# Criss-cross attention on one core: attention matmuls of 96 columns and 96 partitions instead of 128

## The reference

```python
q = jnp.einsum('oc,bchw->bohw', Wq, x) + bq[None, :, None, None]   # 64 channels
k = jnp.einsum('oc,bchw->bohw', Wk, x) + bk[None, :, None, None]   # 64 channels
v = jnp.einsum('oc,bchw->bohw', Wv, x) + bv[None, :, None, None]   # 512 channels
energy_H = jnp.einsum('bchw,bcgw->bhwg', q, k)
energy_H = energy_H - NEG * eye[None, :, None, :]
energy_W = jnp.einsum('bchw,bchv->bhwv', q, k)
att = jax.nn.softmax(jnp.concatenate([energy_H, energy_W], axis=-1), axis=-1)
att_H, att_W = (att[..., :H], att[..., H:])
out_H = jnp.einsum('bcgw,bhwg->bchw', v, att_H)
out_W = jnp.einsum('bchv,bhwv->bchw', v, att_W)
return gamma * (out_H + out_W) + x
```

## Time and profile before

| | |
|---|---|
| median of 2 runs | 4363.76 us (4362.07 to 4365.45) |
| profiled execution, span from first to last instruction | 4357.4 us |
| mean granted TensorE clock | 0.936 |
| TensorE busy with matmuls | 93% of the span |
| weight loads | 84% |
| VectorE, ScalarE, GpSimd busy | 50%, 30%, 26% |
| DMA | 947.78 MB, mean 218 GB/s |

### The profile page before, as it was taken

The page is one execution under the profiler, slowest core; times in us unless marked ns, Lnnn a source line. Parts: engine busy times, 40 slices in busy tenths (PEclk is TensorE's granted clock), DMA queues, the critical chain, the costliest instruction groups (busy, mean ns, idle before and its releaser), DMA issues.

```text
span 4357.4 us, 92393 instructions
## 1 busy us (share of the span) xinstructions
PE 4063.6 (93%) x26136; PEld 3654.3 (84%) x26136; DVE 2184.9 (50%) x3932; ACT 1288.8 (30%) x2522; POOL 1148.6 (26%) x1006
## 2 busy tenths in 40 slices
PE   8989999898998999989999899997999979999897
PEld 7878988788887998879988699886988869988697
DVE  3348533485334853348433484335843358433584
ACT  3342133421334213341133411335113351133510
POOL 3322133221332213322233222332223322233211
PEclk9988999889998999979999799997999979999799
DMA  5548977489774897749977499774997749977499
GB/s 177 172 150 213 247 231 244 153 219 253 232 238 146 222 256 229 247 136 229 249 236 239 136 232 245 246 238 134 234 239 243 240 137 232 252 237 232 148 243 315
DMA packets 555124, 947.78 MB, mean 218 GB/s; under 512 B 45120, under 2 KB 383552, under 8 KB 533568
## 3 DMA queue, kind: packets, MB, share of 16 engines
q1 hardware_dynamic: 555072, 947.30, 75.2%
HBM read 550.77 MB, written 396.36 MB: 217 GB/s over the span
## 4 chain that ended last, share of the span: by engine, by line
PE 82%; DMA 9%; issue 3%; ACT 2%; SPq 1%; POOL 1%; DVE 0%; ACTq 0%; POOLq 0%; DVEq 0%
PE bank L708 36%; PE bank L766 26%; PE bank L724 9%; DMA Pe<-e_scratch 7%; PE bank L745 5%; PE bank L734 3%; PE bank L755 3%; ACT kq L461 1%; DMA KQ<-kq_scratch 1%; POOL Pe L388 1%; ACT E L466 1%; DMA kq_scratch<-kq 1%; POOL x_split L372 0%; SPq L224 0%; DVE X L608 0%
## 5 line engine op out<-in xcount | busy, mean ns | idle before, releaser
L708 PE MATMUL bank<-Wv_hi,x_split 128*128 128x512 f32 x4608 | 1525.6, 399 | 0.0
L766 PE MATMUL bank<-Pt,V 128*128 128x128 f32 x12288 | 1478.4, 280 | 0.0
L766 PEld LDWEIGHTS bank<-Pt,V 128*128 128x128 f32 x12288 | 1436.7, 196 | 0.0
L608 DVE TENSOR_TENSOR X<-bank,X 128x384 f32 (+1 forms) x1536 | 1115.4, 734 | 559.1 <-PE bank L766 559.0
L372 POOL TENSOR_TENSOR x_split<-X,x_split 128x768 fp32r<-128x768 f32 x384 | 702.3, 1854 | 1411.1 <-ACT x_split L435 1411.0
L555 DVE TENSOR_TENSOR v_out<-bank,bv_row 128x512 f32<-128x512 f32 x576 | 398.3, 691 | 1287.3 <-PE bank L708 1281.2
L708 PEld LDWEIGHTS bank<-Wv_hi,x_split 128*128 128x128 f32 x4608 | 867.9, 188 | 189.0 <-issue 0.5
L708 PE MATMUL bank<-Wv_lo,x_split 128*128 128x512 f32 x2304 | 912.5, 396 | 0.0
L388 POOL TENSOR_TENSOR Pe<-Pe,mx 96x384 f32<-96x384 f32 x384 | 316.6, 824 | 1288.6 <-DMA Pe<-e_scratch 1287.8
L474 ACT ACTIVATE Pt<-bank 96x384 f32<-96x384 f32 x384 | 187.3, 488 | 1424.9 <-PE bank L755 1424.9
L446 ACT ACTIVATE kq<-bank,bqk_sb 64x192 f32<-64x192 f32 x768 | 320.6, 417 | 812.1 <-PE bank L734 645.8
(11 more groups left out here) (45 smaller groups left out, 1551.9 us busy)
## 6 DMA issues: line engine op xcount, KB each, us to landing
V<-v_scratch SPq DMA_DIRECT2D x384, 768.0 KB, 5.7
X<-in_x SPq DMA_DIRECT2D x192, 768.0 KB, 5.1
v_scratch<-v_out SPq DMA_DIRECT2D x576, 256.0 KB, 3.8
out<-X SPq DMA_DIRECT2D x192, 768.0 KB, 6.3
Pe<-e_scratch SPq DMA_DIRECT2D x384, 144.0 KB, 5.3
kq_scratch<-kq SPq DMA_DIRECT2D x384, 96.0 KB, 2.3
e_scratch<-E SPq DMA_DIRECT2D x384, 72.0 KB, 1.7
e_scratch<-E SPq DMA_DIRECT2D x192, 144.0 KB, 1.9
```

The costliest lines, as they stand in the source:

```text
L608: nc.vector.tensor_tensor(xs, o_ps[r][:, :].rearrange("p (t n) -> p t n", t=CT)[:, :, 0:N], xs, ALU.add).then_inc(o_added, 1)
L708: last = nc.tensor.matmul(v_ps[t % 2][:, :], x_split[:, j, lo, ct, at], w[:, ct, :], start=(ct == 0 and n == 0), stop=(ct == CT - 1 and n ...
L766: last = nc.tensor.matmul(o_ps[r][:, ct * WIDE:(ct + 1) * WIDE], V[:, c, r, ct * P:(ct + 1) * P], Pt[:, c, r * N:r * N + WIDE], start=True ...
```

## The change

The attention matmuls stream the 96 columns of their own row and contract over the 96 partitions that hold data. The results stand in PSUM without gaps between the four channel tiles, so VectorE reads the first 4 x 96 columns of a bank. What made the padding zero goes, with its semaphores and TensorE's waits for it. `Pt` gets 32 columns narrower per buffer. Nothing else is touched: weight loads, DMAs, their order and the ring stay.

```diff
-WIDE = 128
+WIDE = 96
...
-        pt_padded = sem("pt_padded")
-        v_padded = [sem(f"v_padded{j}") for j in range(RING)]
...
                 mask(b, TRIPLES - 1, 2)
-                nc.gpsimd.memset(Pt[0:N, :, CP:], 0.0).then_inc(pt_padded, 1)
-                nc.gpsimd.memset(Pt[N:P, :, :], 0.0).then_inc(pt_padded, 1)
-                nc.gpsimd.memset(V[N:P, 0, :, :], 0.0).then_inc(v_padded[0], 1)
...
-                for j in (1, 2):
-                    nc.scalar.activation(V[N:P, j, :, :].rearrange("p r c -> p (r c)"),
-                                         kq[N:P, 0, 0:1].to_broadcast((P - N, ROWS * C)), ACT.Copy)\
-                        .then_inc(v_padded[j], 1)
...
-                    nc.vector.tensor_tensor(xs, o_ps[r][:, :].rearrange("p (t n) -> p t n", t=CT)[:, :, 0:N], xs,
+                    nc.vector.tensor_tensor(xs, o_ps[r][:, 0:CT * WIDE].rearrange("p (t n) -> p t n", t=CT)[:, :, 0:N], xs,
                                             ALU.add).then_inc(o_added, 1)
...
                         last = nc.tensor.matmul(o_ps[r][:, ct * WIDE:(ct + 1) * WIDE],
-                                                V[:, c, r, ct * P:(ct + 1) * P], Pt[:, c, r * N:r * N + WIDE],
+                                                V[0:N, c, r, ct * P:(ct + 1) * P], Pt[0:N, c, r * N:r * N + WIDE],
                                                 start=True, stop=True)
...
-                pe.wait_ge(pt_padded, (b + 1) * 2)
-                for j in range(RING):
-                    pe.wait_ge(v_padded[j], b + 1)
                 turn(b, 0, 0, 0)
```

## The result

The changed kernel takes 5583.14 us (median of 2 runs, 5582.21 to 5584.07) where the kernel before takes 4363.76 us: a quotient of 1.279; the ratio on record is 1.281, with a 95% interval of 1.2785 to 1.2834. The profiled execution's span is 5580.4 us, 1223.0 us more than before. 5610 us was forecast, from a sum of 1248 us.

A forecast was written before the change was run, and what follows sets the result against it. TensorE was taken to set the pace, 3.93 us per chunk. Attention at 1.2 GHz adds 1230 us and projections 18 us to the 4357.4 us span: 5605, with 6.4 us to the median 5610 us; 8-in-10 range 4345 to 5680 us.

The forecast's parts named there:

- The load step: Attention: 128-column weight loads pace each record, 0.11 us at full clock, 0.214 us at 1.2 GHz; fewer streamed columns gain nothing.
- The one sure gain: Last matmul of each attention chunk, before a transpose's short load: 0.112 to 0.082 us at full clock, 11.5 us less overall.
- The padding work: Memsets and copies before attention end 0.24 and 0.73 us before the transposes can start; removing them gains nothing.
- One sign given for it: Sign for the padding: attention's first transpose again starts some 0.25 us after the first scaling.
- The clock: Attention enters at 1.2 GHz and stays there until the next batch's projections: 1230 us more over eight batches; chance 0.45.
- Rival A: Attention's clock rises within a few us of entry, loads hold 0.11 us: 4373 to 4456 us, 4394 at two spells; chance 0.39.
- The terms of the sum: Attention at 7.50 us per chunk, 359 us per batch, adds 1230 us; projections starting at the low level add 18 us.
- the start of the projections at the low level: Projections of seven batches begin at 1.2 GHz after attention, losing 2.6 us each: 18 us.
- B: Attention's load does not bind or is shorter, and the clock rises: 0.082 us pace, 4294 us, 4078 without DMA limit; chance 0.06.
- C: Attention at low clock but with shorter loads: streamed columns set 0.164 us per record, 4998 us; chance 0.10 including mixtures.
- A mixture: Clock low in half of the attention stages, landing in C's region, 4998 us; chance 0.10 together with C.

## Why the prediction was right

*The load step* held at both levels: 0.112 us per record with 96 columns in the run that cut the columns alone, the same with 96 columns and 96 partitions at 2.4 GHz, 0.2134 us at 1.2 GHz. A load from 96 partitions might have been shorter, and was not. The Trainium skill ("TensorE: Matmul & The Clock Gate", LDWEIGHTS), by which a load goes with its columns and not with its rows, agrees: 3.57 us for 32 loads from 96 partitions, 0.112 us each.

*The one sure gain*, 0.03 us per chunk at full clock, is there in the run that entered at 2.4 GHz: 32 records and 4 transposes start every 3.90 us (1178.37 to 1182.27), before every 3.93 us. It shows only where the clock is up.

*The padding work* gained nothing, as said: the column energies' last matmul starts at 338.3 and attention's first at 348.8, 10.5 us later; before it was 340.0 and 350.4, 10.4 us. One sign given for it did not come: the first transpose was to start again some 0.25 us after the first scaling.

```profile
344.87 0.82 POOL L386 TENSOR_TENSOR Pe<-Pe,mx 96x384 f32<-96x384 f32 x1 [2.99 <-DVE mx L665]
...
345.75 0.87 PE L745 MATMUL bank<-ident,Pe 96*96 96x96 f32 x4 [0.79 <-POOL Pe L386]
...
348.10 0.88 PE L745 MATMUL bank<-ident,Pe 96*96 96x96 f32 x4 [1.48 <-POOL Pe L386]
```

It starts 0.06 us after (345.75 - 345.69), so about 0.2 us seem to have gone with TensorE's waits for the padding, which the prediction took to be over by then. Nothing came of it, for attention's first matmul stands behind the second chunk's transposes at 348.10, and these wait for a scaling of their own.

*The clock* was the step that decided, and it was argued by resemblance: the new matmuls at 1.2 GHz look more like the column-energy stage than like today's attention. The outcome bears out the value, but not the likeness, and to that extent it was luck, at a chance of 0.45. The column-energy stage streams 96 columns on 128 partitions, with pauses and with 96 columns of weights; attention with 96 streamed columns on 128 partitions, in the run that cut the columns alone, saw the clock rise 5.0 us after the entry. The array standing with nothing streaming for a quarter of the time, which that run has too at the low level, was therefore not enough either. The prediction named 96 columns and 96 partitions in one breath; with either cut alone the clock rose within 5 to 6 us of the entry, and with both it stayed down. Rival A (4373 to 4456 us) was close to right for either half of the change, 4368 and 4379 us. Why it takes both stays open. The rule of the Trainium skill (same page, Part 1) that sustained matmul work raises the clock did not hold for these matmuls: 356 us of TensorE without a pause stayed at 1.2 GHz, eight times. By the Trainium skill (same page, Part 4) transposes do not count as busy in the same way; every attention here has them, so no run shows whether they hinder the rise.

*The terms of the sum.* A chunk is 7.47 us and not 7.50, a batch's attention 356.9 us and not 359: 8 x 356.9 = 2855 us less the 1638 us that the eight lasted before (the prediction's 203.3 and 219.3 us make 1642) gives 1217 us where 1230 stood. The other miss, about as large, is the start of the projections at the low level, put at 18 us by half of today's 5.2 us entry: what is left of the 1223.0 us for it and all else is 6 us. The clock came back 2.6 us after attention's last matmul had started in the first batch (705.7 to 708.3) and 4.4 us after it in the seventh (4881.7 to 4886.1), sooner than the 5.2 us that were taken.

*Rivals B and C.* B's pace of 0.082 us was seen in no run. C's pace of 0.164 us at the low level neither: the loads double with the clock. A mixture, with the clock down in part of the stages, did occur, but only in the run that raised the clock first.

## What to carry to other kernels

Before narrowing a matmul, read which of its two halves sets the pace: with one float32 load of 128 columns per matmul the pace here was 0.11 us for 128 streamed columns and for 96, so cutting the streamed half brought nothing. Padding that costs no time can decide whether TensorE's clock rises, so a change that makes matmuls smaller is judged by the granted clock of their stage, first of all by the level at which the stage is entered; here keeping either half of the padding was within 0.5% of the kernel before. A clock that is low in a stage need not be a loss: the records of the column energies followed each other no faster at 2.4 GHz, though what the whole stage would do there was not separated from the matmuls that held the clock up.

## What the runs showed of the hardware that I had not expected

The level can last: the same stream of matmuls ran at 2.4 GHz before a wait of 7.52 us (TensorE idle for 2.0 us of it) and at 1.2 GHz for 66 us behind it, and whole batches of one execution differ (222 us and 356 us) by whether the clock held through their first microseconds. Work that adds nothing to the result made the difference: with 32 partitions of zeros, or with 32 columns that nobody reads, the clock rose 5.0 and 5.8 us after the entry, and with neither it stayed down for 356 us. And a matmul whose moving operand is read with a stride of 96 float32 values, as KQ is in the column energies, takes 0.16 to 0.17 us at either level, twice the 0.082 us of the transposes' 96 columns at 2.4 GHz; that the stride is the cause was not tried.
